# Order of two scores, two maxima and a sum where cross attention ends and local attention begins

## The reference

```python
x = x + _L0_xattn_ref(_layernorm(x, axis=-1), ctx_1024, L0_xattn_w1_w, ...)
x = x + _L0_attn_ref(_layernorm(x, axis=-1), L0_attn_q_w, L0_attn_q_b, ...)
x = x + _L0_ffn_ref(_layernorm(x, axis=-1), L0_ffn_gate_w, L0_ffn_wg, ...)

# _L0_attn_ref, a block of W = 64 queries sees its own 64 keys and the 64 ahead of it
scores = jnp.einsum('bnqhd,bnkhd->bnhqk', Qb, Kw) / math.sqrt(dh)
rel_ok = (k_idx >= q_idx) & (k_idx <= q_idx + W)
scores = jnp.where(mask[None, :, None, :, :], scores, -jnp.inf)
wts = jax.nn.softmax(scores, axis=-1)
out = jnp.einsum('bnhqk,bnkhd->bnqhd', wts, Vw).reshape(B, N, D)
return out @ o_w.T + o_b
```

## The kernel before

| engine | order |
|---|---|
| TensorE | weigh(14), weigh(15), local_score(0), fused(3), local_score(1), wait x1_ready, project(1,0), local_score(2), project(1,1), turns of unit 0, local_score(3), ... |
| VectorE | probs_low(15), sums (L1073, L1074), copy (L1077), local_max(0), outputs(3), local_max(1), local_sum(0), local_max(2), local_sum(1), local_max(3), ... |
| GpSimd | memset of the values' region (L589, behind the last weigh), then the products by unit |

## Time and profile before

### The profile page before, as it was taken

The page is one execution under the profiler, slowest core; times in us unless marked ns, Lnnn a source line. Parts: engine busy times, 40 slices in busy tenths (PEclk is TensorE's granted clock), DMA queues, the critical chain, the costliest instruction groups (busy, mean ns, idle before and its releaser), DMA issues.

```text
span 598.2 us, 9977 instructions
## 1 busy us (share of the span) xinstructions
PE 571.6 (96%) x3765; PEld 487.6 (82%) x3765; DVE 414.6 (69%) x701; ACT 332.5 (56%) x564; POOL 254.5 (43%) x259
## 2 busy tenths in 40 slices
PE   7799999999999999989999989999999999999995
PEld 5589988998799889967676867888888888888884
DVE  3866686668656865579888688676767676777761
ACT  4337535753476455628766827565647474747450
POOL 6366347534742484334544620333333333333212
PEclk9999999999999999999999989999999999999998
DMA  8993086008600200000002966999999999999642
GB/s 291 424 413 157 1 329 233 1 2 324 239 1 2 71 1 2 1 1 1 2 2 75 397 260 240 339 323 342 332 345 329 339 333 354 337 343 323 226 154 88
DMA packets 25166, 119.27 MB, mean 199 GB/s; under 512 B 2640, under 2 KB 8912, under 8 KB 14096
## 3 DMA queue, kind: packets, MB, share of 16 engines
q1 hardware_dynamic: 20752, 112.48, 49.9%
q0 software_dynamic: 4368, 6.16, 5.3%
HBM read 113.52 MB, written 6.42 MB: 200 GB/s over the span
## 4 chain that ended last, share of the span: by engine, by line
PE 80%; DVE 11%; ACT 2%; issue 2%; POOL 2%; DMA 2%; POOLq 0%; SPq 0%; DVEq 0%; ACTq 0%
PE psum L1653 20%; PE psum L1430 14%; PE psum L1670 13%; PE psum L1384 12%; PE psum L1290 11%; PE psum L1346 2%; DVE head_max L963 2%; DVE region_a L968 1%; DMA region_w<-ctx_cols_dram 1%; PE psum L1528 1%; POOL wide_low L562 1%; DVE wide_low L985 1%; PE psum L1312 1%; PE psum L1392 1%; PE psum L1502 1%
## 5 line engine op out<-in xcount | busy, mean ns | idle before, releaser
L677 ACT ACTIVATE wide_high<-region_a 128x1024 fp32r<-128x1024 f32 (+1 forms) x104 | 105.2, 1011 | 97.7 <-PE psum L1653 90.2
L1120 DVE TENSOR_TENSOR wide_low<-region_a,wide_high 128x1024 fp32r<-128x1024 f32 x92 | 112.4, 1224 | 58.2 <-ACT wide_high L677 58.2
L1670 PE MATMUL psum<-region_a,region_w 128*128 128x256 f32 x368 | 83.3, 379 | 0.0
L1430 PE MATMUL psum<-turned_high,wide_low 128*128 128x256 f32 x256 | 78.6, 307 | 2.9 <-DVE turned_low L1046 2.4
L1046 DVE TENSOR_TENSOR turned_low<-psum,turned_high 128x512 fp32r<-128x512 f32 x64 | 43.7, 690 | 54.2 <-ACT turned_high L677 54.1
L1653 PE MATMUL psum<-wide_low,turned_high 128*128 128x512 f32 x184 | 78.2, 425 | 0.2 <-DVE turned_high L1222 0.2
L1670 PEld LDWEIGHTS psum<-region_a,region_w 128*128 128x128 f32 x368 | 69.7, 190 | 10.0
L1653 PE MATMUL psum<-wide_high,turned_low 128*128 128x512 f32 x184 | 72.5, 394 | 0.0
L1430 PE MATMUL psum<-turned_high,wide_high 128*128 128x256 f32 x256 | 72.2, 282 | 0.0
L1430 PE MATMUL psum<-turned_low,wide_high 128*128 128x256 f32 x256 | 72.1, 282 | 0.0
L1653 PE MATMUL psum<-wide_high,turned_high 128*128 128x512 f32 x184 | 72.1, 392 | 0.0
(11 more groups left out here) (223 smaller groups left out, 1196.3 us busy)
## 6 DMA issues: line engine op xcount, KB each, us to landing
region_a<-up_weights_dram SPq DMA_DIRECT2D x23, 2048.0 KB, 9.1
region_a<-down_weights_dram SPq DMA_DIRECT2D x23, 1024.0 KB, 7.3
region_w<-ctx_cols_dram SPq DMA_DIRECT2D x32, 512.0 KB, 9.3
region_a<-ctx_dram SPq DMA_DIRECT2D x16, 1024.0 KB, 12.2
third_weights<-third_weights_dram SPq DMA_DIRECT2D x1, 1035.0 KB, 26.0
residual<-x_dram SPq DMA_DIRECT2D x4, 256.0 KB, 7.8
sums_by_token<-residual SPq DMA_DIRECT2D x2, 512.0 KB, 9.5
normed_rows<-region_s SPq DMA_DIRECT2D x4, 256.0 KB, 6.6
```

Of the source, the lines that this page charges most:

```text
L677: return nc.scalar.activation(dst, src, ACT.Copy)
L1120: nc.vector.tensor_tensor(w_lo[:, k % RING], group_of(k), w_hi[:, k % RING].bitcast(F32), ALU.subtract).then_inc(low_ready, 1)
L1430: last = nc.tensor.matmul(bank[6 + c][:, 0:NTOK], v[:, value_slot(b, g), k, c * P:(c + 1) * P], p[:, g % 2, k, :], start=g == 0 and k == 0 ...
L1670: last = nc.tensor.matmul(to[:, 0:D], hidT[n][:, ic * P:(ic + 1) * P], rows, start=ic == 0, stop=ic == IC - 1)
```

## The change

The scores of unit 0 move from behind value group 15 of batch 3 to ahead of value group 14. The scores of unit 1 move from behind `fused(3)` to ahead of it. On VectorE `local_max(0)` moves ahead of the sums and the copy, and `local_sum(0)` and `local_max(1)` ahead of `outputs(3)`. Nothing is added or removed.

```diff
+SCORE_AT = PAIRS - 2
@@ VectorE
                     if b + 1 < BATCH:
                         ctx_low(b + 1, 0)
+                    else:
+                        local_max(0)
                     dve.wait_ge(exp_done, b * (TPB * PIECES) + TPB * PIECES)
                     then(nc.vector.tensor_reduce(lsum[:, :], lpart, axis=X_AXIS, op=ALU.add))
                     then(nc.vector.reciprocal(linv[:, :], lsum[:, :]))
@@
                     if b + 1 == BATCH:
-                        local_max(0)
+                        local_sum(0)
+                        local_max(1)
                         outputs(b)
@@
-            local_max(1)
-            local_sum(0)
             local_max(2)
             for n in range(len(WORK)):
@@ TensorE
                     for g in range(PAIRS):
+                        if b == BATCH - 1 and g == SCORE_AT:
+                            pe.wait_ge(masks_ready, 1 + TPB)
+                            pe.wait_ge(proj_out, len(FILLS))
+                            local_score(0)
                         weigh(g)
@@
                     if b + 1 == BATCH:
-                        pe.wait_ge(masks_ready, 1 + TPB)
-                        pe.wait_ge(proj_out, len(FILLS))
-                        local_score(0)
+                        local_score(1)
                         fused(b)
@@
-            local_score(1)
             pe.wait_ge(x1_ready, BATCH + FIRST)
             project_next(1, 0)
             local_score(2)
```

## The result

The changed kernel takes 600.78 us (median of 20 runs) against 599.23 for the kernel before (20 runs); the ratio is 1.0032, with a 95% interval of 1.0018 to 1.0047, so it is slower by 1.9 us (1.1 to 2.8). That ratio is the recorded one of the comparison; the two medians alone would give 1.0026, 1.6 us. Single executions of either kernel spread over 4 to 6 us (596.5 to 600.5 before, 598.7 to 604.3 after). A difference of one or two microseconds is therefore not to be read from two executions: the profiled one of after took 599.61 us, less than that of before with 599.96. What can be compared from one trace to the next is the stage itself, counted from an instruction that the change doesn't touch. I take the start of VectorE's low part of group 15, at 255.48 in the earlier trace rows and at 253.65 after.

A forecast was written before the change was run, and what follows sets the result against it. At the seam after batch 3's cross attention, VectorE's chain and TensorE's program order were taken to run nearly level. Order 1.13, clock fall 1.2, less router 0.9 gave 1.4 us over 600.28: 601.7 us, range 600.3 to 603.0.

The forecast's parts named there:

- The fall of the clock: TensorE's 3.4 us gap ahead of project(1,0) brings the lower clock, costing 1.2 us (0 to 1.7).
- the router's gain: The router's 24 small passes escape the low clock and win 0.9 us (0.9 won to 1.5 lost).
- Unit 0 under the weighing: Batch 3's weighing ends 0.90 us late; local_max(0) is hidden, the copy comes 0.84 us later with 2.40 less behind it.
- The adds 2.04 us late: On VectorE, local_sum(0) and local_max(1) ahead of the residual adds bring x1_ready at 265.24, not 263.20.
- project(1,0) and the scores of unit 2 behind the adds: TensorE empty 3.4 us awaiting the adds; VectorE idle 3.2 us; local_max(2) 1.47 us late, local_max(3) 1.13 us late.
- No slack behind it: After local_max(3), nothing in the rest of the local stage takes the 1.13 us delay back.
- rival 4: The low clock lasts a second stretch of equal length: another 1 to 1.7 us, 603 or more; chance 0.06.
- before the 264.5 named: Sign of being wrong, at the seam on TensorE: project(1,0) starts before 264.5 us.
- the clock at its upper level over the gap: Sign of being wrong: no clock fall over TensorE's gap of 3.4 us ahead of project(1,0).
- the first (fall, no gain from the router): Clock falls at the gap ahead of project(1,0), router gains nothing: 602.3 to 603.1 us; chance 0.25.
- the second (no fall): Clock doesn't fall at the gap ahead of project(1,0): 600.5 to 601.4 us; chance 0.22.
- The third, VectorE's own chain: VectorE's chain sets the seam's end, local_max(2) starting right behind the adds: 1.75 us won, 598.5 us; chance 0.05.

The follow-up runs named there:

- the version with the freed queries: Changed kernel with project(1,0) written to bank 4, so it and unit 2's scores don't wait for the residual adds: 596.96 us, 0.9967 times before.
- the freed queries with the adds first: Changed kernel with project(1,0) in bank 4 and, on VectorE, residual adds back ahead of local_max(1) and local_sum(0): 1.0016 times before.

## Why the prediction was right, and where it wasn't

The forecast was 1.4 us slower, in a range of 600.3 to 603.0 us; measured were 1.9 us (1.1 to 2.8), and 600.78 us. The 601.7 counts from the median of 600.28 of three runs; over 20 runs the kernel before takes 599.23, 1.05 less, which is why 600.78 lies under the forecast although the change costs more than was said. The mechanism of the order held. The fall of the clock came in two of three traces, where the chances added up to 0.73 for it, the router's gain doesn't exist, and that the sum came within 0.5 us is in part luck: the terms partly made up for one another.

1. **Unit 0 under the weighing.** Right to 0.1 us: no wait ahead of group 15, local_max(0) 0.60 us behind the low part (0.62 said), the copy at 3.53 (3.47 said).
2. **The adds 2.04 us late.** Measured 1.85. To the next instruction the copy takes 0.67 rather than 0.75, local_sum(0) 1.37 rather than 1.48, and local_max(1) 2.35 rather than 2.39.
3. **project(1,0) and the scores of unit 2 behind the adds.** This is the step that decides, and it held: a gap of 3.19 us (3.4 said), released by the adds, and VectorE idle for 3.21 us where the clock stayed up (3.2 said). Freeing just this path turned 1.9 us lost into 2.0 won. Without a fall local_max(3) is 0.91 us late, 1.13 was said; the 0.2 are those of step 2.
4. **No slack behind it.** Right: the loss at local_max(3) and at the last unit agree to 0.1 us in every trace of the table.
5. **The fall of the clock, 1.2 us (0 to 1.7).** That the gap brings it is right. The reason given was not: the gap was said to be longer than one without a fall (2.03 us) and one with (2.23). In the second trace of before a fall followed 1.95 us, and in the first of after none followed 2.23, so the length of the idle time alone doesn't decide. (The trace of before also has a third low stretch, from 595.2 us to its end, which was overlooked and lies behind the last matmul.) The price was read as one number, but it is a draw: 0, 1.54 and 2.77 us in three traces. The upper end of 1.7 was too low, because a low stretch may last 6.83 us and not 3.41; I had given that case 0.06 as rival 4, and it is one of three traces. The Trainium skill, "TensorE: Matmul & The Clock Gate", section "Why this matters for your kernels", has an idle gap between bursts put the clock back; the traces agree in two of three at 3.19 us of idle time.
6. **The router's gain of 0.9.** Wrong as a step. The 24 passes took 3.27 us in the one trace of before that I had, and I took this for a property of the kernel that a later arrival would change. In its second trace, with nothing changed, they took 2.59; in the three of the changed kernel 2.85, 2.59 and 3.48. The difference isn't the change's, and the term should have been 0 with a wide range. With it at 0 and the others as said, the sum would have been 2.3; with 0.91 for the order, 2.1, near the 1.9 that came out.

Two of the signs of being wrong need an answer. project(1,0) started at 263.28, before the 264.5 named; but the whole seam lay 1.83 us earlier in this trace, and from the low part of group 15 it is 9.63 us, against 9.82 forecast and 9.02 as the limit, so this sign was badly chosen and shows nothing. The other, the clock at its upper level over the gap, did come true in one of the three traces.

Of the rivals, the first (fall, no gain from the router), the second (no fall) and the fourth (the low stretch twice as long) each have one of the three traces of the changed kernel. The third, VectorE's own chain, failed at the point I gave: it needs the path from the end of the adds to local_max(2) under 1.75 us, and where the clock stayed up that path took 3.2. Taking that path off TensorE's wait is what makes it come true: 598.5 was its price for the median of 600.28, 1.75 us under, and the version with the freed queries is 2.0 under.

## What to carry to other kernels

Before work is moved ahead of a step, list what the other engines have queued behind that step: here 3.9 us of VectorE's work in front of the adds was hidden from VectorE's point of view, but it had been the cover of a TensorE path of 3.2 us behind them. If a reordering opens a wait, ask what the wait is really for; it was for a bank, not for data, and another bank turned the same reordering into a gain. And when one trace has something in it that depends on the clock, take a second trace of the unchanged kernel before you put it into a sum.

## What the hardware showed that I had not expected

- Behind the same gap of 3.19 us, at the same place of the same program, the granted clock fell for 3.41 us, for 6.83 us, or not at all. A wait of 2.42 us was followed by a fall too (the freed queries with the adds first), one of 1.76 us was not. Early in the execution the lengths say even less: in the second trace of before a low stretch followed a wait of 1.95 us,

```profile
19.04 0.50 PE L1384 MATMUL psum<-wide_high,wide_low 128*128 128x512 f32 x1 [1.95 <-DVE wide_low L985]
...
20.29:23.70 3.41, 3.41 (x9) 2.63 (x8) 0.87 (x3) 0.11 (x1) 0.00 (x0) 0.50 1.05 432
```

and in the first of after none followed 2.23 us:

```profile
27.54 0.50 PE L1386 MATMUL psum<-wide_high,wide_low 128*128 128x512 f32 x1 [2.23 <-DVE wide_low L986]
...
27.54:32.04 4.50, 4.50 (x20) 3.73 (x21) 3.31 (x9) 1.06 (x1) 0.00 (x0) 1.00 1.03 424
```

- Elsewhere the low stretches move as well: the early one lay at 28.62 us, at 20.29, or was missing (as in the first trace of after), with the seam 1.8 us earlier for it. The router's 24 small passes took between 2.59 and 3.48 us. Of the 69 executions of the kernel before that ran beside the experiments, 12 of the 13 with a mean granted clock of 0.994 or more took 597.0 to 598.0 us, and 15 of the 16 at 0.986 took 600.6 to 602.0. So much of the spread goes with the clock, but not all: single ones took 604.65 us at 0.994 and 605.23 at 0.990, and what held them up no trace shows.
